# Turning q and x1 for batches 2 to 8: VectorE 32-blocks and on-chip transfers in place of TensorE transposes

## The chip, the core and the metric

The kernel runs on one core of one Trainium2 chip. The metric is the device time of one execution, in microseconds, given as the median of several runs. Five engines work in parallel and meet only through semaphores: TensorE (PE in the rows; PEld is its weight load), VectorE (DVE), ScalarE (ACT), GpSimd (POOL) and SyncE (SP), which here does nothing but issue transfers. Every engine executes its own list of instructions strictly in order, so an instruction that waits holds back all that stands behind it on its engine.

## The reference, cut to what matters

Eight batches of 1024 rows of 256 columns in fp32 go through an attention layer without a softmax over the keys, a layer norm, a feed-forward layer of 16 gated experts, and a second layer norm.

```python
qkv = x @ Wqkv + bqkv                      # x: (8, 1024, 256)
q, k, v = split(qkv);  q -= mean(q);  k -= mean(k)
q2 = q*q;  q2 = l2norm(q2 / (sum(q2) + 1e-7), over the row)
k2 = k*k;  k2 = l2norm(k2 / (sum(k2) + 1e-7), over the 1024 rows)
kv = einsum('bnc,bnd->bcd', k2, v)
t2 = einsum('bnc,bcd->bnd', q2, kv) / sqrt(1024)
x1 = layernorm(x + (v + t2) @ Wln + bln)
sel    = sigmoid(x1 @ expert_sel.T)        # 16 experts
scores = relu(einsum('bsd,edh->bseh', x1, keys))
out    = layernorm(x1 + einsum('bseh,ehv,bse->bsv', scores, values, sel))
```

The normalised q2 is the square of q times one number per row, the query scale.

## The kernel before

**Tiles.** A batch is 8 tiles (T) of 128 rows; four tiles (GT) are a group, so a batch has two groups (G). C = 256 columns are M = 2 blocks of 128. Every matmul product is done in split precision: an operand is kept as a high part (`_h`, written by ScalarE) and a low part (`_l`, the difference, written by VectorE), and `product` (L1205 to L1212) issues three matmuls for each pair of 128-blocks.

**Steps.** The program is one list of steps, `step(it, s)`, for `it` 0 to 7 and `s` 0 to 31, written once per engine and joined by semaphores. Steps 0 to 15 of iteration `it` run the 16 experts on the first group of batch `it`, steps 16 to 31 on its second group. In step s TensorE does 12 up matmuls (`up_bank`, x1 against an expert's keys), then whatever `layer1` has planned for that step, then 12 down matmuls (`down_bank`) of the step before. VectorE makes `gated` from `up_bank` and `sel_all` (L974), ScalarE copies its high part `gated_h` (L501), VectorE makes the low part `gated_l` (L980), and GpSimd spreads the next expert's row of `sel` over the partitions (L487).

**The plan.** The attention part of the next batch is fed into the steps by the table LOOP (L38), an order written out by hand; FIRST and LAST are its versions for the first and the last iteration. Its entries: QK projects q and k of a tile, GG adds to the Gram sum, KS and KV finish the key side, Y makes a tile of the attention output plus x, ZA and ZN finish the output, LG makes the logits of the expert selection for a group. **QT** turns two tiles of q on TensorE: four 128x128 transposes of `q2` against `ident` into a bank of `ring_bank` (L1437), then `qT_h` by ScalarE and `qT_l` by VectorE (L850). **XT** turns one tile of x1 in the same way: two transposes (L1453), `x1T_h` by ScalarE and `x1T_l` by VectorE (L857). LG waits for `x1T_lo` of its group's last tile. An entry's ScalarE and VectorE work stands either late in its own step (`late`) or early in the next (`early`): in each step VectorE runs `early(s)`, the splitting of x (`split_lo`), ZA, the gating L974, `late(s)` and then `gated_l`; ScalarE runs `early(s)`, `gated_h`, `late(s)`.

**Scale.** Before a tile of q is turned, VectorE multiplies it by its query scale (L956, `scale_q`; in the first batch L1001), and Y is one sum in `ring_bank` of an x part (`wvl`) and a q part (`kvw`), to which VectorE adds x (L792).

**Transfers.** All are issued by SyncE, in the order of its list: x and xT of the next batch, rows of `sel` (`move_rows`, L408), stores of `z` (L400). `w_room` (512 KB) is used only for weights while the kernel starts.

Of the kernel before, what the change touches and what calls it, by code (L numbers as in the profile page):

```python
# [5 lines left out]
F32 = mybir.dt.float32  # L6
# [5 lines left out]
P = 128  # L12
# [4 lines left out]
GT = 4  # L17
# [34 lines left out]
    bias_x={9: 0, 14: 1, 28: 2, 30: 3},  # L52
    scale_q={19: (0, 1), 21: (2, 3), 30: (4, 5), 31: (6, 7)},
# [58 lines left out]
def build_program(nc, x, xT, wqk, wvT, wln, b_qk, b_v, b_ln, esel, keys, values, ident_in, out):  # L112
    with ExitStack() as ctx:
# [58 lines left out]

        w_stage = [w_room[:], z[:].rearrange("p a t c -> p (a t c)")]
# [64 lines left out]
        q_scaled = sem("q_scaled")  # L238
# [36 lines left out]
        def q_tile(b, t):  # L275
            return tile(b, t) - GT
# [96 lines left out]
        def _(sp):  # L373
            def load_half(it, h):


                at_least(sp, xT0_lo, T // 2)
                at_least(sp, xT_lo, k_half(it + 1, h) - 1)
                sp.dma_start(xT_raw[:], xT[it + 1, :, h]).then_inc(xT_in, 16)
                at_least(sp, y_added, tile(it, GT * h + GT - 1))  # L380
# [9 lines left out]
            def store_pair(it, goff, p):  # L390
# [9 lines left out]
                sp.dma_start(out_dram[b, :, t:t + 2], z[:, p]).then_inc(stored[p], 16)  # L400
# [1149 lines left out]
```

## Time and profile before

| | us |
|---|---|
| median of 3 runs | 1028.42 (1027.38 to 1028.54) |
| the profiled execution, its own time | 1028.88 |
| its span, first instruction to last | 1027.1 |
| TensorE busy | 1009.6 (98% of the span) |
| VectorE busy | 785.6 (76%) |
| ScalarE busy | 497.3 (48%) |
| GpSimd busy | 213.5 (21%) |

Busy time is the union of an engine's instructions. A matmul's end is modelled and runs into the next one's start (durations of 0.28 us at starts 0.12 us apart), so what a matmul costs TensorE is read from the distance between starts, not from its duration. The transfers of the DMA engines take 8.7% of their time.

### The profile page before, as it was taken

Reading aid. Unit: us, or ns where it says so; the run is one execution under the profiler, and the core shown is the slowest. Engines: PE = TensorE matmul, PEld = TensorE weight load, DVE = VectorE, ACT = ScalarE, POOL = GpSimd, SP = SyncE. Lnnn points to the kernel's source line nnn. Section 1 sums busy time; section 2 is a strip of 40 time slices with the busy share of each in tenths; the row PEclk is TensorE's granted clock in tenths of the full one; section 3 lists DMA queues with packets and bytes.
Section 4 is the critical chain, followed back from the end, with each engine's and each line's share of the span. In section 5 each row is a group of like instructions: output and inputs, shape, how many; then the busy total and the mean of one; then the engine's idle time right before and its main releaser. Section 6 shows DMA issues by size and latency. Waiting matters only on the chain.

```text
span 1027.1 us, 22057 instructions
## 1 busy us (share of the span) xinstructions
PE 1009.6 (98%) x8548; PEld 999.9 (97%) x8548; DVE 785.6 (76%) x1790; ACT 497.3 (48%) x1118; POOL 213.5 (21%) x267
## 2 busy tenths in 40 slices
PE   7899999999999999999999999999999999999996
PEld 6899999999999999999999999999999999999996
DVE  5889876878778887777877878687886878777565
ACT  4555643465435653456524565345553465434332
POOL 0021222212121121212212112221222212122221
PEclk8999999999999999999999999999999999999999
DMA  5031001100011000110001100011000200000000
GB/s 183 22 124 63 3 22 39 65 3 3 22 43 63 3 2 21 44 63 3 18 5 54 53 2 22 1 64 42 3 22 3 83 21 3 22 3 22 3 22 21
DMA packets 13484, 32.83 MB, mean 32 GB/s; under 512 B 1858, under 2 KB 3650, under 8 KB 13380
## 3 DMA queue, kind: packets, MB, share of 16 engines
q1 hardware_dynamic: 13380, 31.42, 8.7%
q8 instruction: 68, 1.11, 0.4%
q14 instruction: 36, 0.29, 0.1%
HBM read 22.50 MB, written 8.39 MB: 30 GB/s over the span
## 4 chain that ended last, share of the span: by engine, by line
PE 95%; DVE 3%; ACT 1%; issue 1%; DMA 0%; POOL 0%; DVEq 0%; POOLq 0%
PE up_bank L1210 34%; PE down_bank L1210 34%; PE ring_bank L1210 9%; PE qk_bank L1210 8%; PE g_bank L1210 4%; PE ring_bank L1437 1%; PE ring_bank L1453 1%; PE ring_bank L1460 1%; PE g_bank L1256 1%; PE ring_bank L1459 1%; PE ring_bank L1422 1%; ACT gated_h L501 0%; DVE gated L974 0%; DVE gated_l L980 0%; DMA sel_all<-in_b_qk 0%
## 5 line engine op out<-in xcount | busy, mean ns | idle before, releaser
L501 ACT ACTIVATE gated_h<-gated 128x512 fp32r<-128x512 f32 x256 | 161.5, 631 | 400.9 <-DVE gated L974 400.9
L487 POOL PARTITION_BROADCAST sel_all<-sel_rows x240 | 196.8, 821 | 704.2 <-DVE gated L974 703.3
L1210 PE MATMUL down_bank<-vals_h,gated_h 128*128 128x256 f32 x1024 | 291.5, 285 | 1.0 <-DVE gated_l L980 0.8
L1210 PE MATMUL up_bank<-x1T_h,keys_l 128*128 128x256 f32 x1024 | 285.0, 278 | 0.0
L1210 PE MATMUL up_bank<-x1T_h,keys_h 128*128 128x256 f32 x1024 | 284.9, 278 | 0.0
L1210 PE MATMUL up_bank<-x1T_l,keys_h 128*128 128x256 f32 x1024 | 284.9, 278 | 0.0
L1210 PE MATMUL down_bank<-vals_l,gated_h 128*128 128x256 f32 x1024 | 284.7, 278 | 0.0
L1210 PE MATMUL down_bank<-vals_h,gated_l 128*128 128x256 f32 x1024 | 284.5, 278 | 0.0
L974 DVE SCALAR_TENSOR_TENSOR gated<-up_bank,sel_all 128x512 f32<-128x512 f32 x256 | 176.1, 688 | 61.3 <-PE up_bank L1210 58.8
L980 DVE TENSOR_TENSOR gated_l<-gated,gated_h 128x512 fp32r<-128x512 f32 x256 | 175.3, 685 | 50.0 <-ACT gated_h L501 48.9
L1210 PEld LDWEIGHTS down_bank<-vals_h,gated_h 128*128 128x128 f32 x1024 | 192.6, 188 | 2.9 <-DVE gated_l L980 1.0
L1210 PEld LDWEIGHTS down_bank<-vals_l,gated_h 128*128 128x128 f32 x1024 | 193.0, 189 | 0.7
L1210 PEld LDWEIGHTS up_bank<-x1T_l,keys_h 128*128 128x128 f32 x1024 | 193.4, 189 | 0.1
L1210 PEld LDWEIGHTS up_bank<-x1T_h,keys_l 128*128 128x128 f32 x1024 | 193.3, 189 | 0.0
L1210 PEld LDWEIGHTS up_bank<-x1T_h,keys_h 128*128 128x128 f32 x1024 | 193.0, 189 | 0.0
L1210 PEld LDWEIGHTS down_bank<-vals_h,gated_l 128*128 128x128 f32 x1024 | 192.8, 188 | 0.0
L1210 PE MATMUL qk_bank<-wqk_h,xT_h 128*128 128x256 f32 x240 | 69.0, 287 | 3.4 <-DVE xT_l L1034 3.3
L1210 PE MATMUL qk_bank<-wqk_l,xT_h 128*128 128x256 f32 x240 | 67.3, 280 | 0.0
L1210 PE MATMUL qk_bank<-wqk_h,xT_l 128*128 128x256 f32 x240 | 67.3, 280 | 0.0
L774 DVE TENSOR_TENSOR qk<-qk_bank,qk_bias 128x512 f32<-128x512 f32 x56 | 38.5, 688 | 31.3 <-PE qk_bank L1210 30.2
L1210 PEld LDWEIGHTS qk_bank<-wqk_h,xT_h 128*128 128x128 f32 x240 | 46.0, 192 | 4.2 <-DVE wqk_l L1026 3.6
L792 DVE TENSOR_TENSOR y<-ring_bank,x_raw 128x256 f32<-128x256 f32 x60 | 25.4, 424 | 28.8 <-PE ring_bank L1210 28.8
(244 smaller groups left out, 1678.5 us busy)
## 6 DMA issues: line engine op xcount, KB each, us to landing
out<-z SPq DMA_DIRECT2D x32, 256.0 KB, 2.4
x_raw<-in_x SPq DMA_DIRECT2D x15, 512.0 KB, 4.8
xT_raw<-in_xT SPq DMA_DIRECT2D x14, 512.0 KB, 3.8
w_room<-in_keys SPq DMA_DIRECT2D x4, 512.0 KB, 4.0
z<-in_values SPq DMA_DIRECT2D x4, 512.0 KB, 3.4
xT_raw<-in_xT SPq DMA_DIRECT2D x4, 256.0 KB, 3.5
sel_rows<-sel SPq DMA_DIRECT2D x64, 8.0 KB
x<-in_wqk SPq DMA_DIRECT2D x2, 256.0 KB, 3.4
```

What stands on the lines that cost most here:

```text
L487: nc.gpsimd.partition_broadcast(sel_all[:, e % 2], row, P).then_inc(sel_spread, 1)
L501: return nc.scalar.activation(dst, src, ACT.Copy, **kw)
L774: V.tensor_tensor(qk[:], qk_bank[:], qk_bias[:], ALU.add).then_inc(qk_biased, 1)
L792: V.tensor_tensor(y[:, a % 2], ring_of(it, s, "Y", a)[:, 0:C], x_raw[:, a], ALU.add).then_inc(y_added, 1)
L974: V.scalar_tensor_tensor(out=gated[:], in0=up_bank[s % 2][:], scalar=0.0, in1=sel_all[:, s % 2], op0=ALU.max, op1=ALU.mult).then_inc(gate_ ...
L980: V.tensor_tensor(gated_l[:, s % 2], gated[:], gated_h[:, s % 2].bitcast(F32), ALU.subtract).then_inc(gated_lo, 1)
L1210: last = mm(dst, lhs, rhs, start=start and i == 0, stop=stop and i == n - 1, **kw)
L1256: last = mm(g_bank[:, m * C:(m + 1) * C], x_raw[:, a, m * P:(m + 1) * P], k0_normal[p % 2][:, i], start=(a == 0 and m == 0), stop=(a == T ...
L1422: last = mm(bk[:, j:j + 2], total[:, m * P:(m + 1) * P], ones[:, 0:2], start=True, stop=True)
L1437: last = nc.tensor.transpose(bk[:, j:j + P], q2[:, 2 * a + i, m * P:(m + 1) * P], ident[:])
L1453: last = nc.tensor.transpose(bk[:, m * P:(m + 1) * P], x1[:, a, m * P:(m + 1) * P], ident[:])
L1459: mm(bk[:], esel_hl[:, m], x1T_h[:, a, m], start=(m == 0), stop=False)
```

## The change

For batches 2 to 8 (index 1 to 7) the entries QT and XT are gone. In their place:

- QS and XS: VectorE turns a whole tile of q2 or x1 in 32x32 blocks with one instruction, out of place, into a quarter of `w_room` (`stage_tile`). After the fourth tile of a group SyncE issues 16 transfers (`turn`), each of 32 partitions by 2 runs of 128 numbers (32 KB), which carry block (i, j) from row group i to row group j: for q back into the group's half of `q2`, for x1 into `z`.
- QR and XR: ScalarE makes the high parts of the turned group in two copies of 128x512, VectorE the low parts in two subtractions of 128x512, now from SBUF and not from `ring_bank`.
- The unscaled q2 is turned. Y keeps its x part in columns 0 to 255 of the bank and its q part in 256 to 511; VectorE applies the query scale to the q part while adding x, in a first instruction, and adds the x part in a second. LIFT moves into `col_scale`.
- `w_room` is one buffer for all four turns of a batch, so a staging waits for the turn before it to have landed. A turn of x1 waits for `z` to be stored; ZA, which writes `z`, waits for `x1T_lo`.
- In the plan Y 0 to 3 stand one step earlier (22 to 25), LG 0 one step later (30), LG 1 two later (12); rows of `sel` for the second group are moved at SyncE's step 14.

```diff
 LOOP = dict(
     plan={
-        0: [("QT", 2)], 1: [("ZA", 0), ("ZA", 1), ("QT", 3)], 2: [("ZN", 0), ("Y", 4)], 3: [("ZN", 1)], 4: [("Y", 5)],
-        5: [("Y", 6), ("XT", 4)], 6: [("Y", 7), ("XT", 5)], 7: [("XT", 6), ("QK", 0)],
...
-        20: [("ZN", 1)], 21: [("KV", 0), ("QT", 0)], 22: [("QT", 1)], 23: [("Y", 0)],
-        24: [("Y", 1), ("XT", 0)], 25: [("Y", 2), ("XT", 1)], 26: [("Y", 3)], 27: [("XT", 2), ("XT", 3)],
-        29: [("LG", 0)],
+        1: [("ZA", 0), ("ZA", 1)], 2: [("ZN", 0), ("Y", 4)], 3: [("ZN", 1), ("XS", 4)], 4: [("Y", 5)],
+        5: [("Y", 6), ("XS", 5)], 6: [("Y", 7), ("XS", 6)], 7: [("XS", 7), ("QK", 0)], 8: [("QK", 1)],
+        9: [("GG", 0)], 10: [("QK", 2), ("GG", 1), ("QS", 0)], 11: [("XR", 1), ("QK", 3), ("QS", 1)],
+        12: [("GG", 2), ("QK", 4), ("LG", 1), ("QS", 2)], 13: [("GG", 3), ("QS", 3)], 14: [("QK", 5)],
...
+        16: [("GG", 5)], 17: [("QR", 0), ("ZA", 0), ("ZA", 1), ("QK", 7), ("QS", 4)],
+        18: [("GG", 6), ("QS", 5), ("QS", 6)], 19: [("KS", 0), ("ZN", 0), ("GG", 7), ("QS", 7)],
+        20: [("ZN", 1)], 21: [("KV", 0)], 22: [("Y", 0)], 23: [("Y", 1), ("XS", 0)], 24: [("Y", 2), ("XS", 1)],
+        25: [("Y", 3), ("XS", 2)], 26: [("XS", 3)], 27: [("QR", 1)], 29: [("XR", 0)], 30: [("LG", 0)],
     },
-    bias_x={9: 0, 14: 1, 28: 2, 30: 3},
-    scale_q={19: (0, 1), 21: (2, 3), 30: (4, 5), 31: (6, 7)},
+    bias_x={9: 0, 14: 1, 27: 2, 28: 3},
...
+            def turn(it, b, kind, h):
+                turned, landed = (turned_q[h], landed_q) if kind == "QS" else (turned_x, landed_x)
+                sp.wait_ge(staged, GT * (park(b, kind, h) + 1))
...
+                for i in range(blocks[1]):
+                    src = w_room[BLOCK * i:BLOCK * (i + 1)].rearrange("c (m j n) -> c m j n", m=M, j=blocks[1])
+                    for j in range(blocks[1]):
+                        dst = turned[BLOCK * j:BLOCK * (j + 1)].rearrange("c (m i n) -> c m i n", m=M, i=blocks[1])
+                        sp.dma_start(dst[:, :, i], src[:, :, j]).then_inc(landed, 16)
...
+                    elif kind == "QR":
+                        act.wait_ge(landed_q, TURN * (move_no(b, a) + 1))
...
+                    elif kind == "XR":
+                        act.wait_ge(landed_x, TURN * (move_no(b, a) + 1))
+                        at_least(act, up_made, (b - 1) * STEPS + (a + 1) * E)
+                        for m in range(M):
+                            copy(quarters(x1T_h[:, a, m].rearrange("p (a n) -> p a n", a=GT)),
+                                 by_tile(turned_x, m)).then_inc(x1T_hi, 2)
...
-                    V.tensor_tensor(y[:, a % 2], ring_of(it, s, "Y", a)[:, 0:C], x_raw[:, a],
+                    V.scalar_tensor_tensor(out=y[:, a % 2], in0=ring_of(it, s, "Y", a)[:, C:2 * C],
+                                           scalar=q_scale[:, a:a + 1], in1=x_raw[:, a], op0=ALU.mult,
+                                           op1=ALU.add).then_inc(y_joined, 1)
+                    dve.wait_ge(y_joined, tile(it + off, a) - GT)
+                    V.tensor_tensor(y[:, a % 2], ring_of(it, s, "Y", a)[:, 0:C], y[:, a % 2],
                                     ALU.add).then_inc(y_added, 1)
...
+            def stage_tile(b, kind, a):
+                k = park(b, kind, a // GT)
...
+                else:
+                    dve.wait_ge(x1_made, tile(b, a))
+                    V.transpose(staged_tiles[:, :, a % GT], x1[:, a]).then_inc(staged, 1)
```

**TensorE, step 27 of an iteration.** Before, the transposes of XT 2 and 3 stand between the last up matmul of the step and the first down matmul:

```order
L1210 MATMUL up_bank<-x1T_l,keys_h 128x256
L1210 MATMUL up_bank<-x1T_h,keys_l 128x256
L1453 MATMUL ring_bank<-ident,x 128x128 [waits x1_made,x1T_lo]
L1453 MATMUL ring_bank<-ident,x 128x128
L1453 MATMUL ring_bank<-ident,x 128x128 [waits x1_made,y_added]
L1453 MATMUL ring_bank<-ident,x 128x128
L1210 MATMUL down_bank<-vals_h,gated_h 128x256 [waits gated_lo]
```

Now steps 26 to 29 have no layer 1 work on TensorE at all, and the first is LG of step 30, behind that step's up matmuls:

```order
L1314 MATMUL up_bank<-x1T_h,keys_h 128x256
L1314 MATMUL up_bank<-x1T_l,keys_h 128x256
L1314 MATMUL up_bank<-x1T_h,keys_l 128x256
L1565 MATMUL ring_bank<-x1T_h,esel_hl 128x512 [waits x1T_lo,y_added]
L1566 MATMUL ring_bank<-x1T_l,esel_h 128x512
```

Of 256 transposes 32 are left (the first batch's); the 8220 other matmuls are the same in number.

**ScalarE, steps 26 to 31.** Before, the copies of x1T (from `ring_bank`) stand three steps ahead of the sigmoid:

```order
L593 ACTIVATE y_std<-y_mv,eps_ln 128x1 [waits y_aggregated]
L501 ACTIVATE gated_h<-gated 128x512 [waits down_made,gate_applied]
L501 ACTIVATE x1T_h<-ring_bank 128x2x128 [waits up_made,x1_transposed] x2
L501 ACTIVATE gated_h<-gated 128x512 [waits down_made,gate_applied] x2
L501 ACTIVATE sel<-ring_bank 16x512 [waits rows_in2,rows_in3,rows_in1,sel_spread,rows_in0,logits_made]
```

Now two copies of the landed group stand between the `gated_h` of steps 29 and 30, and the first of them waits for the transfers:

```order
L550 ACTIVATE gated_h<-gated 128x512 [waits down_made,gate_applied] x2
L550 ACTIVATE qT_h<-q 128x4x128 [waits y_projected,landed_q]
L550 ACTIVATE qT_h<-q 128x4x128
L550 ACTIVATE gated_h<-gated 128x512 [waits down_made,gate_applied] x2
L550 ACTIVATE x1T_h<-z 128x512 [waits up_made,landed_x]
L550 ACTIVATE x1T_h<-z 128x512
L550 ACTIVATE gated_h<-gated 128x512 [waits down_made,gate_applied]
```

The copies have moved from their own steps to one place, one step ahead of LG.

**SyncE, one iteration from its step 2.** Before:

```order
L400 DMA out<-z 128x512 [waits out_made] x2
L379 DMA xT_raw<-in_xT 128x1024 [waits xT_lo,xT0_lo]
L381 DMA x_raw<-in_x 128x1024 [waits y_added]
L408 DMA sel_rows<-sel 4x512 [waits sel_spread,sel_made]
L408 DMA sel_rows<-sel 4x512 x3
```

Now (of these rows the first turn is step 7's, the second step 13's):

```order
L427 DMA out<-z 128x512 [waits out_made] x2
L404 DMA xT_raw<-in_xT 128x1024 [waits xT_lo,xT0_lo]
L408 DMA x_raw<-in_x 128x1024 [waits y_added]
L443 DMA z<-w_room 32x2x128 [waits stored1,stored0,staged]
L443 DMA z<-w_room 32x2x128 x15
L443 DMA q<-w_room 32x2x128 [waits q_fourth,staged]
L443 DMA q<-w_room 32x2x128 x15
L451 DMA sel_rows<-sel 4x512 [waits sel_spread,sel_made]
```

Four such turns of 16 stand in an iteration: at SyncE's steps 7, 13, 19 and 26, the third between the two stores of `z`.

## Rows read from the trace of the kernel before

**Rows 1.** The page's span, busy shares (section 1) and shares of the last chain (section 4).

```profile
span 1027.1 us, 22057 instructions
PE 1009.6 (98%) x8548; PEld 999.9 (97%) x8548; DVE 785.6 (76%) x1790; ACT 497.3 (48%) x1118; POOL 213.5 (21%) x267
...
PE 95%; DVE 3%; ACT 1%; issue 1%; DMA 0%; POOL 0%; DVEq 0%; POOLq 0%
```

**Rows 2.** Waits: engine line waited for, us in total, times, longest.

```profile
DVE gated L974 <- PE up_bank L1210: 58.8, 116, 0.9
```

**Rows 3.** Busy time of iteration 4, 548.55 to 672.40 us: length, then engines, (x instructions).

```profile
548.55:672.40 123.85, 123.85 (x1070) 123.42 (x1069) 96.99 (x224) 61.31 (x140) 26.37 (x33) 1.00 0.08 27
```

**Rows 4.** TensorE's timeline: start us, us; a QT, then an XT.

```profile
514.26 0.60 PE L1437 MATMUL ring_bank<-ident,q 128*128 128x128 f32 x4
...
514.82 0.28 PE L1210 MATMUL down_bank<-vals_l,gated_h 128*128 128x256 f32 x1
...
523.18 0.38 PE L1453 MATMUL ring_bank<-ident,x 128*128 128x128 f32 x2
...
523.52 0.28 PE L1210 MATMUL down_bank<-vals_l,gated_h 128*128 128x256 f32 x1
```

**Rows 5.** TensorE's timeline, up matmuls of steps 27, 28 and 29 of iteration 4.

```profile
657.27 0.28 PE L1210 MATMUL up_bank<-x1T_h,keys_h 128*128 128x256 f32 x1
...
658.33 0.28 PE L1210 MATMUL up_bank<-x1T_h,keys_h 128*128 128x256 f32 x1
...
660.50 0.28 PE L1210 MATMUL up_bank<-x1T_h,keys_h 128*128 128x256 f32 x1
...
661.52 0.28 PE L1210 MATMUL up_bank<-x1T_h,keys_h 128*128 128x256 f32 x1
...
663.22 0.28 PE L1210 MATMUL up_bank<-x1T_h,keys_h 128*128 128x256 f32 x1
...
664.58 0.39 PE L1459 MATMUL ring_bank<-x1T_h,esel_hl 128*128 128x512 f32 x1
```

**Rows 6.** VectorE's timeline in step 27, and ScalarE's `gated_h` of step 29.

```profile
658.89 0.69 DVE L974 SCALAR_TENSOR_TENSOR gated<-up_bank,sel_all 128x512 f32<-128x512 f32 x1 [0.63 <-PE up_bank L1210]
660.28 0.69 DVE L980 TENSOR_TENSOR gated_l<-gated,gated_h 128x512 fp32r<-128x512 f32 x1 [0.70 <-ACT gated_h L501]
...
665.51 0.63 ACT L501 ACTIVATE gated_h<-gated 128x512 fp32r<-128x512 f32 x1 [2.01 <-DVE gated L974]
```

**Rows 7.** SyncE's timeline: transfers issued back to back; one on-chip move; GpSimd behind it.

```profile
9.57 0.60 SPq L428 DMA_DIRECT2D x<-in_wqk  x1
10.21 0.59 SPq L417 DMA_DIRECT2D x_raw<-in_x  x1
10.85 0.43 SPq L414 DMA_DIRECT2D xT_raw<-in_xT  x1
11.33 0.47 SPq L432 DMA_DIRECT2D bv_col<-in_b_v  x1
...
51.37 1.14 SPq L408 DMA_DIRECT2D sel_rows<-sel  x2
...
53.15 1.46 POOL L487 PARTITION_BROADCAST sel_all<-sel_rows  x2 [0.85 <-DMA sel_rows<-sel]
```

**Rows 8.** Groups by form: line, shapes, xcount, busy us, mean ns, idle before.

```profile
L907 DVE SCALAR_TENSOR_TENSOR k_l<-k,k_scale,k_h 128x256 fp32r<-128x256 f32 x56 | 38.2, 681 | 0.0
...
L792 DVE TENSOR_TENSOR y<-ring_bank,x_raw 128x256 f32<-128x256 f32 x60 | 25.4, 424 | 28.8 <-PE ring_bank L1210 28.8
...
L1453 PE MATMUL ring_bank<-ident,x 128*128 128x128 f32 x120 | 21.7, 272 | 0.0
...
L956 DVE TENSOR_SCALAR q<-q,q_scale 128x256 f32<-128x256 f32 x56 | 20.6, 408 | 0.0
...
L938 DVE SCALAR_TENSOR_TENSOR y<-bvl,col_sums,ring_bank 128x256 f32<-128x256 f32 x14 | 6.1, 477 | 4.9 <-PE ring_bank L1210 4.9
...
L912 DVE COPY k_total<-k 128x256 f32<-128x256 f32 x7 | 2.0, 287 | 0.0
```

More of the change, by code:

```diff
@@ L78, in batch_offset @@
         return int(a < T // 4)
-    if kind == "LG":
+    if kind in ("LG", "XR"):
         return 1 - a
@@ L450, in step @@
                     load_half(it, 0)
-                if s == 7 and has(it, 1):
-                    load_half(it, 1)
-                for kind, a, off in planned(it, s, ("LG", "ZN")):
-                    if kind == "LG":
+                if s == 5 and has(it, 1):
+                    load_xT_half(it, 1)
+                if s == 6 and has(it, 1):
+                    load_x_half(it, 1)
+                for kind, a, off in planned(it, s, ("LG", "ZN", "QS", "XS")):
+                    if kind == "LG" and a == 0:
                         move_rows(it, off, a)
-                    else:
+                    elif kind == "ZN":
                         store_pair(it, off, a)
+                    elif kind in ("QS", "XS") and a % GT == GT - 1:
+                        turn(it, it + off, kind, a // GT)
+                if s == ROWS_STEP and it < B:
+                    move_rows(it, 0, 1)
             run(step)
@@ L853, in early @@
                                         ALU.subtract).then_inc(qT_lo, 1)
+                    elif kind == "QR":
+                        for m in range(M):
+                            dve.wait_ge(qT_hi, q_pair(b, 2 * a + m))
+                            at_m = lambda part: quarters(part[:].rearrange("p u v m n -> p (u v) m n")[:, :, m])
+                            V.tensor_tensor(at_m(qT_l), by_tile(turned_q[a], m), at_m(qT_h).bitcast(F32),
+                                            ALU.subtract).then_inc(qT_lo, 1)
+                    elif kind == "XR":
+                        for m in range(M):
+                            dve.wait_ge(x1T_hi, tile(b, GT * a + 2 * m + 1))
+                            at_m = lambda part: quarters(part[:, a, m].rearrange("p (a n) -> p a n", a=GT))
+                            V.tensor_tensor(at_m(x1T_l), by_tile(turned_x, m), at_m(x1T_h).bitcast(F32),
+                                            ALU.subtract).then_inc(x1T_lo, 2)
                     elif kind == "XT":
@@ L883, in add_zs @@
                     at_least(dve, stored[a], it * (16 * G) + off * 16)
+                    if 0 < it < B:
+                        dve.wait_ge(x1T_lo, tile(it, T - 1) if off == 0 else tile(it, GT - 1))
                     if it == 0:
@@ L952, in late @@
                             V.bn_aggr(z_mv[:, a, i], z_stats[:, a, i]).then_inc(z_aggregated, 1)
-                if s in schedule(it)["scale_q"] and has(it, 1):
-                    for t in schedule(it)["scale_q"][s]:
-                        dve.wait_ge(q_scale_set, it + 1)
-                        V.tensor_scalar(q2[:, t], q2[:, t], q_scale[:, t:t + 1], LIFT, ALU.mult,
-                                        ALU.mult).then_inc(q_scaled, 1)
+                for kind, a, off in planned(it, s, ("QS", "XS")):
+                    stage_tile(it + off, kind, a)
+            def stage_tile(b, kind, a):
+                k = park(b, kind, a // GT)
+                if k == 0:
+                    dve.wait_ge(piece_lo, WPIECES - 1)
+                else:
+                    sm, moves = {0: (landed_x, 2 * (b - 1)), 1: (landed_q, 2 * b - 1), 2: (landed_q, 2 * b),
+                                 3: (landed_x, 2 * b - 1)}[k % 4]
+                    dve.wait_ge(sm, TURN * moves)
+                if kind == "QS":
+                    dve.wait_ge(q_squared, k_tile(b, a))
+                    V.transpose(staged_tiles[:, :, a % GT], q2[:, a]).then_inc(staged, 1)
+                else:
+                    dve.wait_ge(x1_made, tile(b, a))
+                    V.transpose(staged_tiles[:, :, a % GT], x1[:, a]).then_inc(staged, 1)
             def weights_lo(i):
```

76 lines of the change are left out of this document (57 added, 19 removed), and 7 rows, old and new, of tables (FIRST_PLAN, plan).

## The prediction

> **What bounds the kernel now.** I read four views. First the page [rows 1]: TensorE is busy 98% of the span and holds 95% of the chain that ended last, VectorE 76%. Second the list of waits: VectorE waits 116 times for TensorE at the gating [rows 2], TensorE hardly for VectorE. Third one iteration by engine [rows 3]: 123.85 us, TensorE busy in all of it, VectorE in 96.99. So time goes only where TensorE has less to issue or newly waits. Fourth the timelines, for the price of a piece of TensorE work [rows 4, 5] and for how far ahead of TensorE its suppliers are [rows 6].
>
> A matmul's duration is no price, its distance to the next start is. In [rows 5] nine up matmuls of 128x256 take 1.06 us in step 27 (0.118 each) and 1.02 in step 28 (0.113). Both paces occur at a granted clock of 1.00 [rows 3]; in this iteration about 370 of the 1038 matmuls that are no transposes go at the slower (start-to-start distances sorted; the rows show one stretch of each). A step of 24 matmuls alone takes 663.22 - 660.50 = 2.72 us at the fast pace, 24 x 0.118 = 2.83 at the slow one.
>
> **What is removed.** A QT: from 514.26 to the second down matmul at 514.82 are four transposes and one matmul, 0.56 us, less 0.118 is 0.44. An XT: 523.52 - 523.18 - 0.118 = 0.22 [rows 4]. The seven batches lose 28 QT and 56 XT: 28 x 0.44 + 56 x 0.22 = 12.3 + 12.3 = **24.6 us**, all of it on the path, as TensorE is the path. An iteration goes from 123.85 to 120.3 us if TensorE never waits.
>
> The mean duration of one transpose is 272 ns [rows 8], but the starts above lie 0.11 us apart, and I price by these. The Trainium skill, page "TensorE: Matmul & The Clock Gate", Part 4, gives about 275 ns for a transpose in one kernel's context and 390 ns alone. The duration agrees; as a price it would make the gain 224 x 0.275 = 62 us, an estimate that the distances of starts contradict.
>
> **What VectorE gains in work, per iteration.** No row of before shows a VectorE transpose. Nearest by shape are the copy of 128x256 in SBUF (287 ns), below, and the k_l operation of 128x256 (681 ns), above; a plain two-input operation of that size takes 424 [rows 8]. I take 0.42: 16 x 0.42 = 6.7 (4.6 to 10.9). The new first instruction of Y, a scalar_tensor_tensor from PSUM, is the same form as L938's, 477 ns: 8 x 0.48 = 3.8. Removed: eight query scales at 408 ns, 3.3. The eight low-part subtractions of x1T at about 0.42 become four of 128x512 at 0.69 [rows 6]: -0.6. For q the four subtractions stay four. Sum +6.6, so VectorE has 103.6 us of work in 120.3 (86%), 108 (90%) with the dear transpose. That fits; what it costs is lateness inside a step, below. ScalarE's four copies for q stay, the eight small ones for x1 become four of 0.63: nothing on the path, except at LG 0.
>
> The Trainium skill, page "VectorE: DVE Perf Modes", section "The three transpose paths", gives 311 ns for 128x128 in bf16 and says that VectorE turns 32x32 blocks only. Two such squares would be 0.62 us per tile, VectorE's work then 107 us an iteration, an estimate inside the bounds above. No run here shows it yet.
>
> **The new wait: LG 0.** This is the dearest part. Time 0 is the start of TensorE's step 26 of an iteration.
> - XS 3 stands behind the gating, which starts 658.89 - 657.27 = 1.62 after its step and takes 0.69 [rows 5, 6]: 2.3, plus 0.42, staged at 2.7.
> - SyncE issues 16 transfers. Plain ones follow each other by 10.21 - 9.57 = 0.64 us or, for a tile in two runs per partition, by 11.33 - 10.85 = 0.48; two on-chip moves take 1.14, 0.57 each [rows 7]. The last is issued 15 distances after the first, and an on-chip move is read 53.15 - 51.37 = 1.78 us after its issue [rows 7]. Landed at 2.7 + 15d + 1.8: 11.7 for 0.48, 12.0 for 0.50, 13.1 for 0.57, 14.1 for 0.64. I take 0.50, by the row of the same shape and a little more for crossing partitions.
> - ScalarE makes gated_h of step 29 first: 3 x 2.83 + (665.51 - 663.22) + 0.63 = 11.4 [rows 5, 6], so it is there in time. Two copies of 0.63 end at 13.3, the second subtraction of 0.69 at **14.0**.
> - TensorE is at LG 0 after four bare steps and twelve up matmuls: 4 x 2.83 + 12 x 0.118 = **12.7**.
>
> TensorE waits 1.3 us. With landing for nothing at 11.4 or before it would be 0.7, with 0.57 it is 2.4, with 0.64 3.4. From 11.4 on, every 0.1 us of later landing costs 0.7 us in all. Seven iterations: **+9.1 us** (5 to 24). Queued behind the wait are LG and every down matmul of step 29; behind ScalarE's wait for the landing stands gated_h of step 30, due at 4 x 2.83 + 2.29 = 13.6, covered by the 13.3.
>
> **The other waits.** The turn of q's second group is read at step 27, of the first at 17, of x1's second group at 11, four or more steps after their stagings: with landing 10 us behind, slack of some us each. What is thin is VectorE's order. Before, gated_l of step 27 ends at 660.28 + 0.69 = 660.97 [rows 6]; its readers stand behind the twelve up matmuls of step 28, at 660.50 + 1.36 = 661.86 [rows 5]: 0.9 us to spare. A transpose and a Y instruction ahead of gated_l (0.42 + 0.48) use up just such a margin. That may happen in some of these steps: 12 and 13 (QS 2, QS 3, LG 1), 18 to 20 (QR 0 ahead of the squares), 22 (Y 0 right behind KV's low part), 28 (both QR subtractions and bias_x). I allow 0.2 us per iteration, **+1.4** (0 to 10). Nothing else costs: the SyncE turns at 7, 13 and 19 delay loads of x and stores by up to 8 us, but these are spread over half an iteration each, and ZA's new waits for x1T_lo fall steps behind it.
>
> **Sum.** 1028.88 - 24.6 + 9.1 + 1.4 = 1014.8 for a profiled execution; the median lies 0.46 below it: **1014.3 us**. A measurement of this kernel can tell about 0.2% (2 us) from no change.
>
> **Rivals.**
> 1. *The full gain.* Both waits vanish: the landing is early enough (transfers on 16 queues overlap, distances under 0.45) and the margins hold. For it: waits of before absorb much, slow-pace matmuls may turn fast as the transposes between them go (370 x 0.0045 = 1.7 us per iteration at most, 12 in all). Against: even a free landing leaves ScalarE's 11.4 + 1.3 + 0.7. Time 1028.4 - 24.6 = 1003.8, with some pace 1000 to 1006.
> 2. *VectorE falls behind.* Transposes cost 0.68 and block gated_l in a dozen steps; TensorE waits 0.1 to 0.2 in each, 1.2 per iteration. For it: VectorE has 3.4 to 4.9 us of work in steps of 3.3 to 4.4 already, and [rows 2] shows that its idle time is mostly a wait for TensorE, thus spread, not saved up. Against: steps 26 to 29 are bare and let it catch up. 1014.3 + 7 x 1.0 = 1021.
> 3. *The transfers are slow,* ending slower than before. One mechanism: 16 issues per turn in a row on SyncE. For it: two rows at 0.64 and the on-chip moves at 0.57. Then the wait at LG 0 is 3.4 at 0.64, which gives 1029; with the landing 1 us longer 1036. It decides from d = 0.65: there the wait eats the whole 24.6 (14.7 us more than forecast, 2.1 per iteration). Against: the row nearest in shape is 0.48. 1030 to 1038.
> 4. *The pace turns.* The transposes go, step lengths change, and the matmuls fall into the 0.118 pace. For it: the same matmuls run at either in neighbouring steps [rows 5], so something small decides. All 668 fast ones of an iteration slow would be 668 x 0.0045 = 3.0 us, 21 in all: 1035; half of it 1024.
> 5. *It does not do what it says* (a staging that waits for a turn of the batch before, say): no gain, 1028.
>
> **How the numbers follow.** Forecast, 1007 to 1020: 0.51. Full gain, below 1007: 0.14. VectorE behind, 1017 to 1025: 0.13. Transfers slow, 1026 to 1038: 0.11. Pace, 1020 to 1035: 0.09, a third of it above 1028. It does nothing: 0.02. The range 1003 to 1027 leaves out most of the third rival, a part of the fourth and the fast end of the first: some 0.17. Faster than 1026.4: 0.51 + 0.14 + 0.13 + 0.01 + 0.07 = 0.86. Within 0.2% (to 1030.5): 0.04. Slower: 0.10.
>
> **What would show it.** TensorE's waits list has a new entry, LG's line for x1T_lo, seven times 1.3 us; none means rival 1, 3 us or more rival 3. SyncE's 16 issues take 8 us and ScalarE's first x1T copy begins at 12.0 on the clock above. The transpose's row gives a mean near 0.42; above 0.6, with down matmuls waiting for gated_l in many steps, it is rival 2. An iteration outside the waits is 120.3 us; longer without waits is rival 4. I am wrong altogether if TensorE waits at a line that I gave slack, above all at QR 0 or at Y.

## The result and the profile after

The changed kernel takes **1062.22 us** (median, 1061.48 to 1063.12), the kernel before 1028.48 beside it: ratio 1.0326, 95% interval 1.0307 to 1.0345. It is 34 us slower, where 14 us faster was forecast. The page of the changed kernel, span, busy shares and last chain, as in [rows 1] (its profiled execution took 1062.88):

```profile
span 1061.0 us, 22202 instructions
...
PE 1009.1 (95%) x8324; PEld 991.4 (93%) x8324; DVE 821.2 (77%) x1874; ACT 495.1 (47%) x1090; POOL 209.9 (20%) x267
...
PE 52%; SPq 17%; DVE 15%; issue 7%; ACT 5%; DMA 4%; DVEq 0%; POOL 0%; ACTq 0%; POOLq 0%
```

TensorE has 224 matmuls fewer (8324 against 8548; the 8292 others, given above as 8220, are the same in number) and is busy as long as before; its share of the chain fell from 95% to 52%, and SyncE, which had none, holds 17%. The list of waits (engine, line, waited for: us in total, times, longest) has what [rows 2] had not:

```profile
PE ring_bank L1565 <- DVE x1T_l L941: 27.4, 8, 4.8
ACT x1T_h L550 <- DMA z<-w_room: 22.3, 8, 4.2
DVE w_room L1061 <- DMA q<-w_room: 10.0, 7, 1.8
PE down_bank L1314 <- DVE gated_l L1084: 6.8, 12, 1.4
DVE w_room L1058 <- DMA z<-w_room: 6.0, 6, 1.4
```

L1565 is LG. One of its waits, in the chain of iteration 3 (start us, us, what), from VectorE's last staging to TensorE:

```profile
547.32 0.45 DVE w_room L1061
547.78 0.59 SPq L443
548.41 0.60 SPq L443
...
556.74 0.60 SPq L443
557.38 1.87 DMA z<-w_room
559.32 0.64 ACT x1T_h L550
560.05 0.47 DVE x1T_l L941
560.53 0.09 issue
560.66 0.69 DVE x1T_l L941
561.36 0.14 issue
561.49 0.47 PE ring_bank L1565
```

Sixteen transfers are issued 0.64 us apart and take 9.6 us from the first issue to the last; the last lands 1.87 us behind. That is the pace of the three turns ahead of LG 0 with the shortest waits (3.14 to 3.16 us). In the other four one or two of the fifteen distances were 0.93 to 1.90 us, and the waits 3.43 to 4.82 us; SyncE's rows of the turns of iterations 0, 1 and 3:

```profile
161.73 11.84 SPq L443 DMA_DIRECT2D z<-w_room  x16
...
289.77 11.00 SPq L443 DMA_DIRECT2D z<-w_room  x16
...
547.78 10.20 SPq L443 DMA_DIRECT2D z<-w_room  x16
```

What held these single issues up is open. TensorE's timeline of iteration 3 shows where it stood, and that its matmuls come back at another distance:

```profile
558.06 0.28 PE L1314 MATMUL up_bank<-x1T_h,keys_l 128*128 128x256 f32 x1
561.49 0.47 PE L1565 MATMUL ring_bank<-x1T_h,esel_hl 128*128 128x512 f32 x1 [3.16 <-DVE x1T_l L941]
...
562.72 0.41 PE L1314 MATMUL down_bank<-vals_h,gated_h 128*128 128x256 f32 x1
562.94 0.42 PE L1314 MATMUL down_bank<-vals_l,gated_h 128*128 128x256 f32 x1
```

Matmuls of 128x256 now start 0.22 us apart (562.72 to 562.94). Windows of this stretch, columns as in [rows 3]: the iteration, the wait, the stretch behind it, the next step.

```profile
441.32:568.18 126.86, 122.75 (x1038) 121.38 (x1037) 102.06 (x235) 61.15 (x136) 25.97 (x33) 0.99 0.15 43
558.06:561.49 3.43, 0.27 (x3) 0.10 (x2) 1.44 (x3) 1.15 (x2) 0.00 (x0) 1.00 0.08 17
561.49:565.50 4.01, 4.01 (x18) 3.75 (x18) 1.74 (x3) 3.13 (x4) 0.00 (x0) 0.59 0.02 4
565.50:568.18 2.68, 2.68 (x24) 2.68 (x24) 0.69 (x1) 0.43 (x1) 1.18 (x2) 0.98 0.03 9
```

The granted clock is 0.59 in the 4 us behind the wait and 0.50 from 562.3 to 565.5: most of them at 1.2 GHz instead of 2.4. **So the wait is paid twice**, 3.3 us of standing and 1.7 us of half speed. Fourteen down and up matmuls at 0.21 instead of 0.11 cost 1.4 us, the four wide ones of LG 0.3. The mean granted clock of the whole span is 0.980, against 0.994 before.

**Where 58 us went** (34 slower instead of 24.6 faster), summed over the starts of all matmuls of iterations 0 to 7 in the two profiled executions:

| | us |
|---|---|
| transposes gone, as forecast | -24.6 |
| TensorE idle as the trace shows it, 35.7 against 1.4; LG makes 27.4 (25.5 at LG 0, 1.9 at LG 1 of the last batch), and 1.4 is one stop at 55.7 us, such as e5 has too (1.3) | +34.3 |
| 32 more stops, 0.16 us each hidden in the modelled end of the matmul ahead | +5 |
| matmuls at the low clock behind a wait (those 0.2 us and more apart) | +12 |
| 3440 matmuls at the 0.118 pace against 2953, 4.5 ns each | +2 |
| rest: stops below 0.16 us, which show as no idle at all (48 more distances of 0.14 to 0.26 us at full clock) | +5 |
| sum | +34 |

The three VectorE terms of the forecast, by form:

```profile
L862 DVE SCALAR_TENSOR_TENSOR y<-ring_bank,q_scale,x_raw 128x256 f32<-128x256 f32 x60 | 28.8, 481 | 14.0 <-PE ring_bank L1314 14.0
...
L1061 DVE STREAM_TRANSPOSE w_room<-x 128x256 f32<-128x256 f32 x56 | 24.2, 432 | 10.2 <-DMA q<-w_room 10.0 <-issue 0.2
L1058 DVE STREAM_TRANSPOSE w_room<-q 128x256 f32<-128x256 f32 x56 | 23.4, 427 | 6.0 <-DMA z<-w_room 6.0
```

### The profile page after: what moved, and what is told of

Its sections match the earlier page's. It is cut to its first block, busy times and chain, and to the rows that moved or that the text cites. A ratio compares the mean times of both kernels' runs of the same rounds, so it can differ in the third digit from the quotient of the medians.

```text
span 1061.0 us, 22202 instructions
## 1 busy us (share of the span) xinstructions
PE 1009.1 (95%) x8324; PEld 991.4 (93%) x8324; DVE 821.2 (77%) x1874; ACT 495.1 (47%) x1090; POOL 209.9 (20%) x267
## 4 chain that ended last, share of the span: by engine, by line
PE 52%; SPq 17%; DVE 15%; issue 7%; ACT 5%; DMA 4%; DVEq 0%; POOL 0%; ACTq 0%; POOLq 0%
PE down_bank L1314 18%; PE up_bank L1314 18%; SPq L443 16%; PE ring_bank L1314 6%; PE qk_bank L1314 5%; DVE gated L1078 2%; DVE gated_l L1084 2%; PE g_bank L1314 2%; DVE x1T_l L941 1%; DMA z<-w_room 1%; ACT gated_h L550 1%; DVE w_room L1058 1%; DMA q<-w_room 1%; DVE w_room L1061 1%; DMA sel_rows<-sel 1%
## 5 line engine op out<-in xcount | busy, mean ns | idle before, releaser
L1314 PE MATMUL down_bank<-vals_l,gated_h 128*128 128x256 f32 x1024 | 288.0, 281 | 0.0
L1314 PE MATMUL down_bank<-vals_h,gated_l 128*128 128x256 f32 x1024 | 287.9, 281 | 0.0
L1084 DVE TENSOR_TENSOR gated_l<-gated,gated_h 128x512 fp32r<-128x512 f32 x256 | 172.6, 674 | 57.9 <-ACT gated_h L550 57.2
L1314 PEld LDWEIGHTS down_bank<-vals_h,gated_h 128*128 128x128 f32 x1024 | 196.0, 191 | 15.8 <-DVE gated_l L1084 12.0
L1314 PEld LDWEIGHTS down_bank<-vals_l,gated_h 128*128 128x128 f32 x1024 | 196.1, 191 | 1.0
L1314 PEld LDWEIGHTS down_bank<-vals_h,gated_l 128*128 128x128 f32 x1024 | 196.1, 191 | 0.0
L550 ACT ACTIVATE k_h<-k,k_scale 128x256 fp32r<-128x256 f32 x56 | 28.6, 512 | 41.0 <-DVE k_scale L903 40.6
```

Source lines behind the costliest of these rows:

```text
L550: return nc.scalar.activation(dst, src, ACT.Copy, **kw)
L1084: V.tensor_tensor(gated_l[:, s % 2], gated[:], gated_h[:, s % 2].bitcast(F32), ALU.subtract).then_inc(gated_lo, 1)
L1314: last = mm(dst, lhs, rhs, start=start and i == 0, stop=stop and i == n - 1, **kw)
```

## The experiments

Theory A: sixteen issues in a row make LG 0 late, and the clock falls behind that wait. Theory B: VectorE's longer work is what costs. Theory C: the pace of the remaining matmuls turns slow once the transposes are gone. All times are medians beside the kernel before on the same chip; "slow" counts matmuls 0.116 to 0.122 us behind the one ahead, in iterations 0 to 7 of the one profiled execution, so it tells of that execution and not of the median. e1_few8, e2_few12, e5, e7 and e8 leave out or misplace a part of the data, as their texts say; they are for measuring only.

| | us | ratio to before (95%) | wait at LG, us | slow |
|---|---|---|---|---|
| before | 1028 to 1031 | 1 | 0 | 2953 |
| the change | 1062.2 | 1.033 (1.031 to 1.035) | 27.4 | 3440 |
| e1_few8 | 1034.6 | 1.004 (1.003 to 1.005) | 5.1 | 4197 |
| e2_few12 | 1029.0, one run | | 9.6 | 3247 |
| e3_one_run | 1062.9 | 1.031 (1.028 to 1.034) | 25.3 | 5034 |
| e4_x_half_on_pe | 1030.5 | 1.000 (0.999 to 1.002) | 2.7 | 4905 |
| e5_before_fewer_transposes | 1024.5 | 0.995 (0.993 to 0.996) | 0 | 4416 |
| e6_act_issues_4 | 1034.1 | 1.004 (1.002 to 1.006) | 6.5 | 2920 |
| e7_four_issues | 1025.6 | 0.995 (0.993 to 0.997) | 4.2 | 4464 |
| e8_four_issues_bias | 1020.7 | 0.992 (0.990 to 0.995) | 4.1 | 3205 |
| e9_four_issues_whole | 1030.5 | 1.001 (1.000 to 1.003) | 5.1 | 5503 |
| e10_rephased | 1033.4 | 1.005 (1.003 to 1.006) | 4.8 | 4087 |
| e11_before_vector_transposes | 1031.1 | 1.002 (1.001 to 1.004) | 0 | 3211 |
| **e12_cheap_q** | **1019.9** | **0.989 (0.988 to 0.991)** | 4.4 | 3616 |
| e13_q_alone | 1023.1 | 0.992 (0.991 to 0.993) | 0 | 3597 |

### Fewer transfers: is it the landing?

```diff
                     for j in range(blocks[1]):
+                        if (kind, h) == ("XS", 0) and 4 * i + j >= 8:      # 12 in e2_few12
+                            continue
```

> Of the sixteen transfers of the turn of x1's first group (the one that LG 0 waits for) only eight are issued, so half of that group's x1T is old data; all else is the changed kernel. Theory A (the sixteen issues in a row, 0.64 us apart, make LG 0 late, and the clock falls behind that wait): the last transfer lands 8 x 0.64 = 5.1 us sooner, before ScalarE is free; the seven idle stretches of 3.1 to 4.8 us shrink below 0.8, no matmuls at half clock behind them, about 1062 - 21 - 12 = 1029 us (1020 to 1033). Theory B (VectorE's 16 transposes and 8 Y instructions make gated_l late everywhere): within 5 us of 1062.

> Twelve of the sixteen transfers of that turn are issued, so a quarter of the first group's x1T is old data. Theory A: landing 2.6 us sooner, idle at LG 0 of 0.6 to 2.2 us. If the fall of the clock needs a wait of about 3 us, it stays at full speed: 1062 - 18 - 12 = 1032 us. If any wait brings it, 1044. Theory B: within 5 us of 1062.

TensorE's wait for x1T_l in the two, e1_few8 first:

```profile
PE ring_bank L1571 <- DVE x1T_l L947: 5.1, 8, 1.7
```

```profile
PE ring_bank L1571 <- DVE x1T_l L947: 9.6, 8, 1.9
```

Theory B falls as the main cause: leaving out four transfers of this one turn takes some 33 us off (a single execution, but far outside the 1061 to 1063 us of the changed kernel). The wait shrinks from 27.4 to 9.6 us, and the stretches at low clock behind LG 0 go with it; in e2_few12 after a wait of 1.94 us the clock stays:

```profile
172.30:174.24 1.94, 0.00 (x1) 0.04 (x1) 1.44 (x3) 0.92 (x2) 0.00 (x0) 1.00 0.00 0
174.24:177.00 2.76, 2.76 (x20) 2.58 (x21) 1.39 (x3) 2.17 (x3) 0.00 (x0) 1.00 0.00 0
```

But e1_few8 missed its own range (1020 to 1033), and with the landing out of the way the kernel is where it was before the change, not 20 us below. The 24.6 us have gone elsewhere: its trace has some 18 us more of stops than before, each counted with its hidden 0.16 us, and 1244 more slow matmuls (5.6 us). It is also slower than e2_few12, whose waits are longer; 950 slow matmuls more (4.3 us) go with that. Its seven remaining waits of 0.5 us at LG 0 are ScalarE's two copies (the 0.7 of the forecast's chain).

### What is the 0.64 us the price of?

```diff
-        staged_tiles = w_room[:].rearrange("p (j a n) -> p j a n", j=C // BLOCK, a=GT)
+        staged_tiles = w_room[:].rearrange("p (j m a n) -> p m j a n", j=P // BLOCK, m=M, a=GT)
-                        sp.dma_start(dst[:, :, i], src[:, :, j]).then_inc(landed, 16)
+                        sp.dma_start(dst[:, i], src[:, j]).then_inc(landed, 16)
```

> All sixteen transfers, with the two 128-blocks of a 32-block column side by side in w_room and in the target, so that each transfer is 32 partitions by one run of 256 numbers instead of two runs of 128. Same bytes, half the packets, same number of issues. If the 0.64 us between issues is the price of the second run: 0.48 apart, landing 2.4 us sooner, idle at LG 0 under 2 us, 1030 to 1045 us. If it is the price of an issue whatever its shape: spacing 0.64, 1060 to 1063. Theory B: no change either.

> All transfers, in one run per partition as in e3_one_run, but of the turn of x1's first group ScalarE issues four of the sixteen itself, in step 26 behind its gated_h; SyncE issues twelve. The output is whole. Theory A: landing 2.6 us sooner than in e3_one_run, as with twelve transfers; idle at LG 0 1 us or less, no low clock; 1028 to 1034 us, if four issues on ScalarE (2.6 us) do not delay gated_h of step 27 by more than 0.4 us. Rival: the two queues share what takes the 0.64 us, the spacing doubles while both issue, and the time stays at 1050 to 1062.

e6_act_issues_4 is e3_one_run and:

```diff
+                    elif kind == "XS" and a == GT - 1:          # ScalarE, step 26
...
+                        for j in range(n):
+                            nc.scalar.dma_start(dst[:, n - 1], src[:, j]).then_inc(landed_x, 16)
```

> Each turn is four transfers instead of sixteen: row group i of w_room, 32 partitions by four runs of 256 numbers, goes to all 128 partitions, with channel 32j + c on partition 4c + j. The weights are not permuted to match, so the channels are contracted in a wrong order; work, bytes and packets are those of the changed kernel. Theory A: a turn lands 12 x 0.64 = 7.7 us sooner, no wait at LG 0 but for ScalarE's two copies (0.5), none for a landed turn at XS 0 or LG 1; no low clock; 1062 - 26 - 12 - 3 = 1021 us, more only by the slow pace (C: up to 1030). If a transfer to 128 partitions costs four times the issue: no change, 1062.

Its tiles lie in `w_room` as in e3_one_run, and:

```diff
                 for i in range(blocks[1]):
-                    for j in range(blocks[1]):
-                        dst = turned[BLOCK * j:BLOCK * (j + 1)].rearrange("c (m i n) -> c m i n", m=M, i=blocks[1])
-                        sp.dma_start(dst[:, :, i], src[:, :, j]).then_inc(landed, 16)
+                    dst = turned.rearrange("p (i n) -> p i n", i=blocks[1])[:, i]
+                    sp.dma_start(dst, src).then_inc(landed, 16)
```

The timeline of SyncE's queue, one turn of x1's first group in e3_one_run:

```profile
549.04 10.02 SPq L443 DMA_DIRECT2D z<-w_room  x16
```

in e6_act_issues_4, SyncE's and ScalarE's:

```profile
533.43 7.72 SPq L445 DMA_DIRECT2D z<-w_room  x12
```

```profile
533.44 2.71 ACTq L637 DMA_DIRECT2D z<-w_room  x4
```

and in e7_four_issues:

```profile
532.64 2.50 SPq L442 DMA_DIRECT2D z<-w_room  x4
```

One run per partition instead of two: 10.02 against 10.20 us. A quarter of the transfers with four times the bytes each, to 128 partitions: still 0.63 each. Two queues at once: each at its own distance; SyncE's twelve take 7.72 us, about what they would alone, ScalarE's four 2.71, their starts 0.55, 0.90 and 0.65 apart. The price is one of the single issue, 0.63 to 0.64 us on SyncE, whatever it carries here, and the spacing does not double while both issue, which was the rival. That decides the layout: a turn must be few transfers. Reading a row group's 32 partitions as 32 x 4 runs and writing them on 128 partitions needs four instead of sixteen. It lands in 1.9 + 2.7 us instead of 9.6 + 1.9, and all waits for a landing are gone from the list. The time, 1025.6, is 4.6 us over theory A's 1021 and within what theory C allowed; its profiled execution has 1024 more slow matmuls than the changed kernel's, as many us. e6_act_issues_4 (1034.1, the upper end of its forecast) has the landing of e2_few12, and pays for it: gated_h of step 27 is 0.5 us late (stops of 0.8 us in place of 0.54 at step 29).

### The stops of 0.54 us

> As e7_four_issues, and the two additions of the output bias to x (bias_x, 0.69 us each on VectorE) moved from steps 27 and 28 to 30 and 31, where they stood near before. Theory A: the seven stops of 0.54 us ahead of the down matmuls of step 29 go, 7 x 0.7 = 5 us less than e7_four_issues. If the time stays, those stops are not on the path.

```diff
-    bias_x={9: 0, 14: 1, 27: 2, 28: 3},
+    bias_x={9: 0, 14: 1, 30: 2, 31: 3},
```

1025.6 became 1020.7: the forecast 5 us. The two intervals (0.993 to 0.997 and 0.990 to 0.995) overlap, so the traces decide. TensorE's wait for `gated_l`, e7_four_issues first:

```profile
PE down_bank L1313 <- DVE gated_l L1083: 5.6, 9, 1.3
```

```profile
PE down_bank L1313 <- DVE gated_l L1083: 2.1, 2, 1.3
```

All seven stops of step 29 are gone: 3.5 us of idle, 4.6 with the hidden parts. In the changed kernel, two low-part subtractions of q and this addition stand ahead of the gating of step 28, and the down matmuls of step 29 wait for it.

### Half the transposes, and VectorE alone

> The kernel before, with only the first transpose of each QT and XT of batches 2 to 8 (84 of 224 stay), so most of q's and x1's turned tiles are old data; nothing else is changed. 140 transposes at the 0.11 us of the prediction are 15.4 us of 24.6. Theory A (a transpose costs TensorE its 0.11 us, no more and no less): 1030 - 15.4 = 1014.5 us (1012 to 1017) when the kernel before is at 1030. Theory C (part of what the transposes cost comes back as a slower pace of the other matmuls, 0.1178 us apart instead of 0.1133, since nothing flips the pace back): 1018 to 1024, with well over 3000 matmuls at the slow pace against 2953.

```diff
-                        for i in range(2):
-                            for m in range(M):
+                        for i in range(1 if b else 2):          # QT; XT likewise
+                            for m in range(1 if b else M):
```

> One part of the change alone: the kernel before, whole, with sixteen VectorE transposes of a constant 128x256 tile into w_room in each of iterations 1 to 7, in the steps and the place where the changed kernel has its own; nobody reads them and nobody waits for them. +48 us of work on VectorE. Theory A (VectorE has the room; a transpose ahead of gated_l stops TensorE only where several pieces meet): 0 to 0.5 us per iteration, 1030 to 1034 us. Theory B (this is what eats the 24.6 us): 1040 or more.

```diff
+                # COUNT: the number in each step, as in the changed kernel
+                if 0 < it < B:
...
+                    for n in range(COUNT.get(s, 0)):
+                        V.transpose(w_room[:].rearrange("p (j a n) -> p j a n", j=8, a=GT)[:, :, n], out_bias[:])
```

e5 is the second surprise. 140 transposes less should give 15.4 us and give 6.3. Its slow matmuls rise from 2953 to 4416 (1463 x 4.5 ns = 6.6 us), and TensorE has 5 us of new stops, among them 0.44 to 0.53 us seven times where a down product now comes before VectorE has added z. e11 says that VectorE's 46 us of extra work by itself cost 2 us (0.5 to 3.7), with no new stop of TensorE. So B is false for the work as such; Y's new instruction was not in this run.

The pace is seen in the whole e12_cheap_q, steps 4 to 8 of iterations 2 and 3, which hold the same 182 matmuls without a wait and at full clock:

```profile
313.19:333.59 20.40, 20.40 (x182) 20.40 (x181) 18.79 (x46) 10.62 (x25) 4.74 (x6) 1.00 0.32 98
435.18:456.38 21.20, 21.20 (x182) 21.20 (x181) 18.70 (x46) 10.66 (x25) 4.60 (x6) 1.00 0.34 100
```

How long a slow stretch lasts differs with XT. In iterations 1 to 6 of the ten traces that have no XT in steps 5 to 8 (the change, e1 to e4, e6 to e9, e12), 33 iterations are slow in step 5, and all 33 still in step 11; of the 13 slow ones of before, e11 and e13, which have XT there, none is; in e5, with half of each XT, two of five. Whether a stretch starts is another matter: of the six iterations one is slow in step 5 in e2 and e6, all six in e3. So the counts of the table run from 2920, below that of before, to 5503 among kernels with the same few transposes, and the pace is no fixed price of taking them away. That is theory C, and it was tried directly.

### The whole computation with four issues

> The whole computation with four transfers per turn. VectorE reads the columns of a 128-block in the order 4c + j (stride 4), so that channel 4c + j stands on partition c of block j, and a transfer of 32 partitions by 4 runs to 128 partitions puts it on partition 4c + j, where the weights want it. bias_x in steps 30 and 31. Work on every engine is that of e8_four_issues_bias except for VectorE's strided reads. If these cost nothing: the time of e8_four_issues_bias, 0.992 of the kernel before, 1018 to 1025 us, faster than both kernels. If a strided read makes a transposition of 0.43 us cost 0.8: 1025 to 1032.

```diff
-                    V.transpose(staged_tiles[:, :, :, a % GT], q2[:, a]).then_inc(staged, 1)
+                    V.transpose(staged_tiles[:, :, :, a % GT], spread(q2[:, a])).then_inc(staged, 1)   # x1 likewise
+            def spread(row):
+                return row.rearrange("p (m c j) -> p m j c", m=M, j=P // BLOCK)
```

> e9_four_issues_whole with two 128x128 transposes of the identity, which nobody reads, ahead of the Y product of tiles 5 and 7 (steps 4 and 6) in seven batches: 28 transposes, +3.1 us of work on TensorE. Theory C (the transposes of before flipped the pace of the matmuls back to 0.113; without them a slow stretch lasts from step 2 to step 12): in the iterations that are slow there the pace flips to fast at step 4 or 6, up to 8 steps x 30 x 4.5 ns = 1.1 us each, so 0 to 4 us faster than e9_four_issues_whole, and no iteration slow all through steps 4 to 12. Rival: the flips of before came from something else; 3 us slower, stretches as before.

```diff
+                        if b > 0 and a in (5, 7):
+                            for m in range(M):
+                                nc.tensor.transpose(bk[:, m * P:(m + 1) * P], ident[:], ident[:])
```

> e9_four_issues_whole with q's columns dealt out in the weights (the projection's columns and its bias are handed over in another order; the squares of the first batch are written back in the old one), so that VectorE's eight transposes of q per iteration read without a stride: 0.43 us instead of 0.62, 1.5 us less VectorE work an iteration, x1's eight stay strided. If VectorE's work is what is left: 3 to 6 us faster than e9_four_issues_whole, 1024 to 1027 us. If it is the pace: within 2 us of it, by how many matmuls are slow (4.5 ns each).

```diff
+    w = np.concatenate([dealt(w[:, 0:C]), w[:, C:]], axis=1)
+    b = np.concatenate([dealt(b[0:C]), b[C:]])
-                    V.transpose(staged_tiles[:, :, :, a % GT], spread(q2[:, a])).then_inc(staged, 1)
+                    V.transpose(staged_tiles[:, :, :, a % GT], q2[:, a]).then_inc(staged, 1)
```

The groups of e12_cheap_q, where x1 is read with a stride of 4 and q without:

```profile
L1062 DVE STREAM_TRANSPOSE w_room<-x 128x256 f32<-128x256 f32 x56 | 35.0, 625 | 0.3 <-issue 0.3
...
L1059 DVE STREAM_TRANSPOSE w_room<-q 128x256 f32<-128x256 f32 x56 | 23.3, 424 | 0.0
```

A stride of four words makes a VectorE transposition 0.20 us dearer. e9_four_issues_whole, with both strided, came out at 1030.5, in the range that its text gave for a transposition of 0.8, though it cost 0.62: nothing is left of the gain. With q's cheap (e12_cheap_q) the kernel is at 0.989, the fastest of those that do the whole computation, and the step is larger than either of the two forecasts (3 to 6 us, or within 2). q's eight stand in steps 10 to 19, which are VectorE's fullest, x1's in the emptier ones; that this is why q's stride costs 1.2% and x1's (e8_four_issues_bias has neither, and the same ratio) nothing is argued, not shown. The two profiled executions lie 12.7 us apart (1035.1, e9's slowest, and 1022.4); 1887 more slow matmuls are 8.5 us of that, stops about 3. So the traces put most of the difference down to the pace, and no run shows whether the pace has anything to do with the stride.

e10_rephased did flip the pace: in iterations 1 to 6 no stretch that was slow in step 5 reached step 11, where in e9 all five did, though in two iterations a new one began in step 7; 4087 matmuls are slow against 5503. Yet its median is 3 us above e9's, what 28 transposes cost, and not 0 to 4 below. So transposes do disturb the pace, which is no use as a cure, and the size of theory C's share stays uncertain, since the counts of single executions vary (e7_four_issues ran from 1020 to 1029 us).

### q's half alone

> q's half of the change alone, in its cheap form: q turned by VectorE and four transfers per turn, query scale on Y's q part; x1 turned by TensorE in the steps of before, LG 0 in step 29, LG 1 in 10. 112 transposes go from TensorE, 12.3 us. VectorE: +8 transposes (3.4), +8 Y instructions (3.8), -8 scales (3.3) an iteration. Theory A: stops of 0.3 to 0.6 us an iteration, 1029 - 12.3 + 3 = 1020 (1017 to 1023), faster than both kernels. Theory C: x1's transposes still stand in steps 5 to 8 and flip the pace back, so the slow matmuls stay near 3000 and nothing more is lost.

```diff
-        25: [("Y", 3), ("XS", 2)], 26: [("XS", 3)], 27: [("QR", 1)], 29: [("XR", 0)], 30: [("LG", 0)],
+        26: [("Y", 3)], 27: [("XT", 2), ("XT", 3)], 29: [("LG", 0)], 30: [("QR", 1)],
```

8.4 of 12.3 us arrive (0.992). Iterations 1 to 7 have one stop of 0.07 us (0.23 with its hidden part) that before had not; the slow matmuls rose to 3597 in spite of x1's transposes, 2.9 us of the 3.9 missing. All six stretches slow in step 5 ended before step 11, as C says; but more of them started, so the forecast that the count stays near 3000 was wrong.

> x1's first group goes back to TensorE (XT 0 to 3 in steps 24 to 27, LG 0 at step 29 as before the change); q and x1's second group stay with VectorE and the transfers. Theory A: 28 XT come back at 0.22, +6.2 us, the waits for the landing (26 us) and the low clock (12 us) go: about 1030 us (1020 to 1036). Theory B: VectorE loses only 4 of its 16 transposes an iteration, so 1050 or more.

```diff
-        25: [("Y", 3), ("XS", 2)], 26: [("XS", 3)], 27: [("QR", 1)], 29: [("XR", 0)], 30: [("LG", 0)],
+        25: [("Y", 3), ("XT", 1)], 26: [("XT", 2)], 27: [("QR", 1), ("XT", 3)], 29: [("LG", 0)],
```

This one has sixteen issues per turn, but no turn ahead of LG 0: 32 us come back, as A says, and all that is left of the gain, 18.4 us, is gone again: 4905 slow matmuls are 8.8 us more than before, and stops some 8 us with their hidden parts, the longest the one of 2.7 us at LG 1 of the last batch, whose steps are short.

## Why the prediction was wrong

**The miss in all.** The forecast for a profiled execution was 1014.8, measured are 1062.9. Of the 48 us between them the wait at LG 0 makes about 18 (26.6 with hidden parts for 9.1), matmuls at the low clock 12, the other stops 16 (for 1.4), the pace 2.

**What bounds the kernel**: right. TensorE's waits, clock and pace account for what was measured.

**What is removed**: right in size as far as the runs can tell; wrong in that it was booked as net. e5 gets 6.3 us for 15.4 of transposes, since the rest of TensorE's list does not stay as it was. The forecast had the pace as rival 4, at 0.09; in the changed kernel itself it made 2 us, in e4 and e7 7 to 9.

**VectorE's work**: right. 0.43 us for a transposition (0.42 taken), 0.48 for Y's first instruction, 102 us an iteration for 103.6. The Trainium skill's 311 ns per 128x128 square in bf16, from the page "VectorE: DVE Perf Modes", section "The three transpose paths", would be 0.62 us for a tile of two squares, an estimate; the trace has 0.43 for the fp32 tile without a stride.

**The wait at LG 0**: the mechanism, place and chain were right, and the term for the distance between issues failed. 0.50 us was taken from a load in two runs per partition; two loads of the same [rows 7] had 0.64, and 0.64 it was. The 0.57 for on-chip moves was misread as well: 1.14 is the length of a merged row, from the first start to the second's end, and these starts lie 0.62 apart (51.37 and 51.99; 0.55 in the median of such moves in that trace). By the prediction's own sum that gives a landing at 14.1, x1T_lo at 16.1 and a wait of 3.4; measured from the start of step 26 (544.95) are 14.3, 16.4 and, from 558.17, when TensorE was through with the up matmuls, 3.3. That the last agrees is in part luck: TensorE came at 13.2 and not at 12.7, held up by the stop in step 29, and its next matmul started 0.1 us behind x1T_lo. Multiplied by fifteen, an uncertainty of 0.14 us was worth 14.7 us in all, and the chance of 0.11 for it was too small with half of the rows in its favour. The single distances of 0.93 to 1.90 us in four of the seven turns add another 3.4 us, and no row of before that the prediction used has one.

**What follows a wait**: missing altogether. Nothing in the prediction has the clock falling, because the kernel before never let TensorE stand for 3 us in its iterations. It made 12 us, and with it rival 3 would have read 1041, not 1029. Even the rival's far end (1038) left out what came behind six of the seven waits.

**The other waits**: 0.2 us an iteration were allowed, and the steps named. Two places were right (the work of step 28 ahead of the down matmuls of 29; 12 and 13, whose stops in 13 and 14 are below 0.16 us but for 0.03 to 0.05 of idle). One had been given slack: VectorE's stagings wait for the turn before to land, 10.0 us at XS and 6.0 at QS in the list above, and behind XS 0 TensorE stops 0.08 to 0.32 us in step 24 in five iterations. Another was not seen, 0.15 us in step 1 where a down matmul waits for `z` (idle in five iterations). The size was wrong everywhere: 0.54 + 0.16 at step 29 alone, seven times, about 2 us in all per iteration. I had taken the margin of 0.9 us from step 28 as it was, without moving two q subtractions and bias_x ahead of its gating; in e8 the seven stops are gone, and 5 us with them.

## What to carry to other kernels

Price a chain of transfers by the number of issues times the dearest distance that the trace shows, read from start to start and not from a merged row, and look for a layout that needs fewer, larger ones. When work leaves an engine that is the bound, its neighbours' margins shrink by as much: sum them per step before booking the gain, and count a new wait of some microseconds on TensorE dearer than its length. Then measure the part that is saved by itself: here 6.3 of 15.4 us arrived in e5 and 8.4 of 12.3 in e13.

## What the runs showed of the hardware

- An issue on SyncE's queue costs 0.63 to 0.64 us for SBUF to SBUF moves of 32 KB (one or two runs per partition, to 32 partitions) and of 128 KB (to 128 partitions) in the change, e3 and e7; single ones took up to 1.9 us, in four of the seven turns ahead of LG 0. On ScalarE's queue in e6 they were 0.55 to 0.90 apart. The last of a turn mostly lands 1.8 to 1.9 us (32 KB) or 2.6 to 3.0 us (128 KB) after its issue; single ones took 3.6 and 4.0. Source and destination may spread the same sequence over different numbers of partitions (e9, e12).
- In the changed kernel TensorE's clock fell to half, for 3 to 6 us, behind six of the seven waits of 3.1 to 4.8 us at LG 0, and stayed behind one of 3.43. In e3_one_run it fell behind all seven, of 2.9 to 4.0 us. It stayed in e2_few12 behind 1.94 us, in e3 behind 1.96, in e6_act_issues_4 behind 2.05 and in e4_x_half_on_pe behind 2.7, but fell in the changed kernel 1.5 us behind one of 1.86 us at LG 1 of the last batch. So no length alone decides, and what does is open. The Trainium skill describes such a clock gate on the page "TensorE: Matmul & The Clock Gate", Part 1; the rows here show both levels, 1.00 and, in the stretch of 0.59, 0.50.
- Matmuls of 128x256 run at one of two paces at full clock, 0.113 or 0.118 us, for ten steps on end and more, and the same program falls into either from iteration to iteration. Transposes in steps 5 to 8 went with an end of every slow stretch there (13 of 13), and without them none of 33 ended before step 11. Executions of e7_four_issues differ by 0.8%; that the pace is what differs is likely, not shown. What starts the slow pace wasn't found.
- VectorE turns 128x256 fp32 in 32-blocks in 0.43 us, with an input stride of 4 words in 0.62 (e12_cheap_q, both in one trace).
